# Decoder layer on one core: the causal mask of the maxima moves from a matmul into VectorE's reduction, and the heads' own blocks are masked on VectorE

## The chip, the cores and the metric

The kernel runs on one core of a Trainium2 chip. The metric is the device time of one execution in microseconds (us), the median of several runs. A core has five engines, each with a queue of its own that is worked off in order: TensorE (PE in the profile; PEld is its loading of weights), VectorE (DVE), ScalarE (ACT), GpSimd (POOL) and SyncE (SP), which here only starts transfers (DMAs). They wait for each other by semaphores. SBUF is the working memory, PSUM the one that matmuls write, in eight banks of 512 float32 columns.

## The reference

One decoder layer over x [8, 512, 256]: attention over tokens, attention over heads within each token, and a linear layer, each behind a layer norm and added to x. The weights' quantisation and the low-rank part belong to the linear layer and are not touched here.

```python
# 1. causal attention over tokens, 16 heads; real and imaginary halves together make 32 dimensions
scores = (q_r @ k_r^T + q_i @ k_i^T) / sqrt(16)
scores = where(tril(ones(N, N)), scores, -inf)
probs  = softmax(scores);  out = probs @ v;  x = x + out @ Wo
# 2. attention over the heads of one token, with q = layernorm(x), k = v = ctx
scores = einsum('bsqd,bskd->bsqk', qh, kh) / sqrt(16)          # 16 x 16 for each token
scores = where(tril(ones(16, 16)), scores, -1e18)
x = x + softmax(scores) @ vh
# 3. x = x + layernorm(x) @ w + bias + low rank part
```

## The kernel before

Eight batches (N_BATCH) of 512 tokens go through a software pipeline. The body is written out for the first turns and the last, and is a loop for those between; each turn has four passes `g`, one for each group of G = 4 heads, and each pass has ten units `n`. All engines run the same `body(i, g, n)` order, each with its own part. In one pass TensorE works on several groups at once: it projects q and k of group A (three ahead), takes the maxima of group B (two ahead, shifted by SHIFT = 1 unit, so that the last unit of a group falls to n = 0 of the next pass), turns the maxima of group M, and computes the exponentials' scores and the weighted values of group C. Batch-wide work (output projection, transposes, layer norms, the linear layer) is hung on single passes, so that one pass in four is longer.

The softmax needs the largest score of each query before the exponentials. So scores are computed twice. For the maxima, queries lie on the partitions: a unit of `QUERY_UNITS` fills one bank of 512 columns with one block of 512 (four units), two blocks of 384 and 128 (four units) or two of 256 (two units). At the end of each unit one more matmul adds the mask: `mask_q` (through the unit matrix `ident_b`, bf16) is added to the one or two diagonal blocks of 128 columns. The function is `scores`, L589 to L604, used for both sides. VectorE then takes the maxima, `take_max`, L1190 to L1201: one TENSOR_REDUCE for each bank. Since a bank with blocks of 384 and 128 columns is reduced in four segments of 128, the three parts of block 2 go to `seg_max`, and after the last unit VectorE waits for itself, joins them by a small reduction (L1259) and a copy (L1260), and tells TensorE by `max_ready`. TensorE turns the 16 maxima of each query into rows (`turn_maxima`, L626), ACT copies them to `max_row` (L943), and a DMA puts them as an extra row into `stack_q`. There are two banks for the maxima (`max_bank0`, `max_bank1`), and TensorE waits with unit n until VectorE has taken unit n - 2.

The operands of both score matmuls lie in `stack_q` and `stack_k`. They are filled by six DMAs of 256 KB for each group from SyncE's queue (L443 to L461): q_hi twice, q_lo, k_hi twice, k_lo, where ACT copies the high part from PSUM and VectorE makes the low part (`low_part`, L1203 to L1208). TensorE waits for all six before unit 0.

The attention over heads is spread over GpSimd and VectorE, a tile of 128 tokens a pass (26 tiles in this way, the others in the end part). GpSimd multiplies (L311), VectorE sums into `head_scores` (L1213, at n = 5 and n = 8), GpSimd adds `head_mask` over 256 columns into `head_probs` (L1580), VectorE takes `head_max` (L1330, n = 9), GpSimd subtracts it (L1583), ACT exponentiates (L931), VectorE sums and inverts, GpSimd normalises (L1565) and multiplies with the values (L1570), VectorE sums and adds to x2 (L1296).

## Time and profile before

| | |
|---|---|
| median of 3 runs | 827.26 us (824.56 to 828.38) |
| profiled execution, its own time | 829.26 us |
| its span, first to last instruction | 827.4 us |
| granted TensorE clock, mean | 0.971 of full speed |
| PE busy | 759.1 us (92%) |
| DVE busy | 628.8 us (76%) |
| POOL busy | 489.6 us (59%) |
| ACT busy | 402.8 us (49%) |

The profile shows one execution. Busy time is the union of an engine's instructions. Matmuls are pipelined and their ends are modelled, so a busy TensorE isn't TensorE at its peak; the distance from the start of one matmul to the start of the next says more. The first 44 us are start-up, the maxima of groups are taken from 34 to 697 us, and the last 100 us are the end part of the last batches.

### The profile page before, as it was taken

Reading aid. Unit: us, or ns where it says so; the run is one execution under the profiler, and the core shown is the slowest. Engines: PE = TensorE matmul, PEld = TensorE weight load, DVE = VectorE, ACT = ScalarE, POOL = GpSimd, SP = SyncE. Lnnn points to the kernel's source line nnn. Section 1 sums busy time; section 2 is a strip of 40 time slices with the busy share of each in tenths; the row PEclk is TensorE's granted clock in tenths of the full one; section 3 lists DMA queues with packets and bytes.
Section 4 is the critical chain, followed back from the end, with each engine's and each line's share of the span. In section 5 each row is a group of like instructions: output and inputs, shape, how many; then the busy total and the mean of one; then the engine's idle time right before and its main releaser. Section 6 shows DMA issues by size and latency. Waiting matters only on the chain.

```text
span 827.4 us, 15883 instructions
## 1 busy us (share of the span) xinstructions
PE 759.1 (92%) x5563; PEld 520.8 (63%) x5563; DVE 628.8 (76%) x1225; ACT 402.8 (49%) x760; POOL 489.6 (59%) x452
## 2 busy tenths in 40 slices
PE   3688999999999999999999999999999998998997
PEld 2565655765566556666666666665766564587995
DVE  2544555457768998899879987999798879789873
ACT  5114555555555566545646573647464546541111
POOL 5000000031966799678958786878787888976541
PEclk9658999999999999999999999999999999999997
DMA  5886656866686668566646675667566760100001
GB/s 180 111 105 82 98 78 84 135 84 84 84 135 78 90 84 134 70 91 107 90 94 90 103 93 100 90 104 95 76 87 107 100 93 8 58 14 8 32 14 38
DMA packets 47980, 70.54 MB, mean 85 GB/s; under 512 B 4897, under 2 KB 22578, under 8 KB 47922
## 3 DMA queue, kind: packets, MB, share of 16 engines
q1 hardware_dynamic: 46898, 69.52, 56.1%
q8 instruction: 34, 0.56, 0.4%
q10 hardware_dynamic: 1024, 0.26, 0.1%
q14 instruction: 24, 0.20, 0.1%
HBM read 14.98 MB, written 4.19 MB: 23 GB/s over the span
## 4 chain that ended last, share of the span: by engine, by line
PE 58%; DMA 15%; DVE 13%; POOL 5%; issue 4%; ACT 2%; SPq 1%; DVEq 0%; ACTq 0%; POOLq 0%
PE misc L518 21%; DMA stack_k<-k_lo 14%; PE exp_bank L518 14%; PE acc_bank L518 9%; PE max_bank L518 9%; PE sum_bank L518 3%; POOL prod L1570 3%; DVE neg_max L1201 2%; DVE seg_max L1201 2%; DVE x L1296 2%; SPq L449 1%; POOL prod L311 1%; DVE head_scores L1213 1%; DVE head_out L1213 1%; DVE ln_raw L1179 1%
## 5 line engine op out<-in xcount | busy, mean ns | idle before, releaser
L927 ACT ACTIVATE probs<-exp_bank 128x512 f32<-128x512 f32 x320 | 188.4, 592 | 204.0 <-PE exp_bank L518 201.1
L1201 DVE TENSOR_REDUCE neg_max<-max_bank 128x1 f32<-128x512 f32 (+1 forms) x192 | 130.6, 683 | 93.0 <-PE max_bank L518 92.4
L1570 POOL TENSOR_TENSOR prod<-head_probs,ctx_sb 128x256 f32<-128x256 f32 (+1 forms) x100 | 185.1, 1882 | 2.2 <-POOL head_probs L1565 0.5
L518 PE MATMUL max_bank<-stack_k,stack_q 96*128 96x384 f32 (+3 forms) x512 | 158.2, 372 | 17.2 <-DMA stack_k<-k_lo 9.1
L518 PE MATMUL acc_bank<-probs,values 128*32 128x512 f32 (+3 forms) x1024 | 157.6, 445 | 4.6 <-ACT log_sum L938 2.6
L311 POOL TENSOR_TENSOR prod<-x1n,ctx_sb 128x256 f32<-128x256 f32 (+1 forms) x104 | 158.4, 1554 | 4.3 <-ACT x1n L887 4.3
L518 PE MATMUL sum_bank<-probs,ones 128*32 128x512 f32 (+3 forms) x1024 | 156.9, 442 | 0.0
L518 PE MATMUL exp_bank<-stack_q,stack_k 97*128 97x384 f32 (+3 forms) x512 | 150.0, 355 | 2.1 <-DVE wf_lo L1171 1.3
L1512 POOL TENSOR_TENSOR ln_var<-ln_mv,eps 128x4 f32<-128x4 f32 x21 | 4.5, 213 | 198.3 <-DVE ln_mv L1187 198.3
L518 PEld LDWEIGHTS exp_bank<-stack_q,stack_k 97*128 97x128 f32 x512 | 84.1, 194 | 56.2 <-issue 28.2
L1201 DVE TENSOR_REDUCE seg_max<-max_bank 128x4 f32<-128x512 f32 x128 | 86.7, 682 | 28.2 <-PE max_bank L518 27.0
L518 PEld LDWEIGHTS max_bank<-stack_k,stack_q 96*128 96x128 f32 x512 | 88.8, 204 | 23.4 <-DMA stack_k<-k_lo 8.6
L518 PE MATMUL max_bank<-mask_q,ident_b 128*128 128x256 bf16 (+1 forms) x320 | 86.7, 271 | 0.0
L518 PE MATMUL exp_bank<-mask_k,ident_b 128*128 128x256 bf16 (+1 forms) x320 | 84.8, 265 | 0.0
L1213 DVE TENSOR_REDUCE head_scores<-prod 128x64 f32<-128x1024 f32 (+1 forms) x104 | 79.6, 805 | 4.0 <-POOL prod L311 4.0
L1213 DVE TENSOR_REDUCE head_out<-prod 128x64 f32<-128x256 f32 (+2 forms) x100 | 74.7, 804 | 0.0
L518 PE MATMUL misc<-xt_hi,w_hi 128*128 128x512 f32 x128 | 57.8, 451 | 14.8 <-ACT max_row L880 12.5
L518 PEld LDWEIGHTS acc_bank<-probs,values 128*32 128x32 f32 x1024 | 39.0, 108 | 45.3 <-issue 27.0
L518 PE MATMUL exp_bank<-prod,ident 128*128 128x160 f32 (+4 forms) x416 | 61.0, 307 | 2.4 <-POOL prod L356 2.4
L518 PEld LDWEIGHTS exp_bank<-prod,ident 128*128 128x128 f32 x416 | 58.9, 190 | 4.0 <-POOL prod L356 2.5
L518 PEld LDWEIGHTS exp_bank<-mask_k,ident_b 128*128 128x128 bf16 x320 | 31.3, 98 | 36.6 <-issue 26.2
L518 PE MATMUL misc<-wo_sb,attn_t 128*128 128x256 f32 x224 | 51.3, 382 | 1.4 <-DVE xt_lo L1312 1.3
(181 smaller groups left out, 1360.2 us busy)
## 6 DMA issues: line engine op xcount, KB each, us to landing
stack_q<-q_hi SPq DMA_DIRECT2D x64, 256.0 KB, 5.6
stack_k<-k_hi SPq DMA_DIRECT2D x64, 256.0 KB, 9.6
stack_q<-q_lo SPq DMA_DIRECT2D x32, 256.0 KB, 7.0
stack_k<-k_lo SPq DMA_DIRECT2D x32, 256.0 KB, 10.7
x_in<-in_x SPq DMA_DIRECT2D x9, 512.0 KB, 4.7
ctx_sb<-in_ctx SPq DMA_DIRECT2D x32, 128.0 KB, 3.3
x<-in_x SPq DMA_DIRECT2D x7, 512.0 KB, 10.1
out<-y_sb SPq DMA_DIRECT2D x5, 512.0 KB, 3.3
```

Of the source, the lines that this page charges most:

```text
L311: last = engine.tensor_tensor(qk_prod[:, COFF[j]:COFF[j + 1]].rearrange("p (q k d) -> p q k d", q=4, d=HD), x1n[:, t, 4 * j * HD:4 * (j + ...
L449: sp.dma_start(to[n * D:(n + 1) * D, s, :, :].bitcast(F32), part[:, :].bitcast(F32)).then_inc(stacked, 16)
L518: return nc.tensor.matmul(*args, **kw)
L927: nc.scalar.activation(probs[:, (UNITS * g + n) % PTR, :], exp_bank[n % 2][:, :], ACT.Exp, scale=SCALE).then_inc(exp_done, 1)
L1179: last = vec.bn_stats(ln_raw[:, which, t, :], src[:, t, :])
L1201: vec.tensor_reduce(o, v, axis=AX_X, op=ALU.max, negate=True).then_inc(max_taken, 1)
L1213: last = vec.tensor_reduce(out(j), products(j), axis=AX_X, op=ALU.add)
L1296: vec.tensor_tensor(x2[:, t, :], x2[:, t, :], head_out[:, :], ALU.add).then_inc(x2_ready, 1)
L1512: own(gp.tensor_tensor(ln_var[:, which, :], ln_mv[:, which, :, 1], eps[:, :], ALU.add))
L1570: last = gp.tensor_tensor(pv_prod[:, COFF[j]:COFF[j + 1]].rearrange("p (q d k) -> p q d k", q=4, k=keys), head_probs[:, 4 * j:4 * j + 4, N ...
```

## The change

The mask matmul of the query side goes. `take_max` now has one instruction for each block: it adds `causal` (zeros, with the triangle in the last 128 columns) to the block, writes the sum back to the bank and keeps the maximum, straight into `query_max`. `seg_max`, the small reduction, the copy and `max_ready` go; the maxima are no longer negated, and ACT's copy to `max_row` gets scale -1. In the attention over heads the entries of later chunks of keys hold the mask's value from the start, and VectorE adds the mask to the heads' own 4 x 4 blocks (`own_heads`, 64 columns) where GpSimd added it over all 256.

```diff
-            def scores(bank, unit, lhs, rhs, slot, rows, key_side, done):
+            def query_scores(bank, unit, slot):
+                for h, blk, at, width in unit[0]:
+                    last = mm(bank[:, at:at + width], stack_q[0:STACK, slot, h, blk * P:(blk + 1) * P],
+                              stack_k[0:STACK, slot, h, 0:width], start=True, stop=True, skip_group_check=True)
+                last.then_inc(max_scored, 1)
+            def key_scores(bank, unit, slot):
                 parts, (col, count, step) = unit
                 for n, (h, blk, at, width) in enumerate(parts):
-                    first = blk * P if key_side else 0
-                    mm(bank[:, at:at + width], lhs[0:rows, slot, h, blk * P:(blk + 1) * P],
-                       rhs[0:rows, slot, h, first:first + width], start=(n == 0), stop=False,
+                    mm(bank[:, at:at + width], stack_k[0:STACK + 1, slot, h, blk * P:(blk + 1) * P],
+                       stack_q[0:STACK + 1, slot, h, blk * P:blk * P + width], start=(n == 0), stop=False,
                        skip_group_check=True)
...
             def turn_maxima(slot):
-                pe.wait_ge(max_ready, n_max_ready.up())
+                pe.wait_ge(max_taken, n_max_ready.up(UNITS))
...
-                            copy(max_row[:, m_slot % 2, :], misc[0][0:G * NT, 0:P]).then_inc(max_row_ready, 1)
+                            nc.scalar.activation(max_row[:, m_slot % 2, :], misc[0][0:G * NT, 0:P], ACT.Identity,
+                                                 scale=-1.0).then_inc(max_row_ready, 1)
...
             def take_max(n, ring):
-                dve.wait_ge(max_scored, n_scored.up())
+                wait_apart(dve, const_ready, (max_scored, n_scored.up()))
                 bank = max_bank[n % 2]
-                if n < G:
-                    o, v = neg_max[:, ring, n:n + 1, 3], bank[:, :]
-                elif n < 2 * G:
-                    o, v = seg_max[:, n - G, :], bank[:, :].rearrange("p (s k) -> p s k", k=P)
-                else:
-                    h = 2 * (n - 2 * G)
-                    o, v = neg_max[:, ring, h:h + 2, 1], bank[:, :].rearrange("p (s k) -> p s k", k=2 * P)
-                vec.tensor_reduce(o, v, axis=AX_X, op=ALU.max, negate=True).then_inc(max_taken, 1)
+                for h, blk, at, width in QUERY_UNITS[n][0]:
+                    v = bank[:, at:at + width]
+                    last = vec.tensor_tensor_reduce(v, v, causal[:, T - width:T], 1.0, -3.0e38, ALU.add, ALU.max,
+                                                    query_max[:, ring, h, blk:blk + 1])
+                last.then_inc(max_taken, 1)
...
-                            if unit == UNITS - 1:
-                                dve.wait_ge(max_taken, n_scored.now())
-                                vec.tensor_reduce(neg_max[:, ring, :, 2], seg_max[:, :, 0:3], axis=AX_X, op=ALU.min)
-                                vec.tensor_copy(neg_max[:, ring, :, 0], seg_max[:, :, 3]).then_inc(max_ready, 1)
...
                             dve.wait_ge(hqk_prod, n_prod.up())
-                            wait(dve, h_masked, n_masked.up() - 1)
+                            wait(dve, h_shifted, n_shifted.up() - 1)
                             score_sums((3,))
...
+                        if scored and n == 9:
+                            dve.wait_ge(hqk_sum, n_masked.up())
+                            vec.tensor_tensor(own_heads, own_heads, head_mask[:, None, 0:4, 0:4]
+                                              .to_broadcast([P, CHUNKS, 4, 4]), ALU.add).then_inc(h_masked, 1)
...
-                            vec.tensor_reduce(head_max[:, :], head_probs[:, :, :], axis=AX_X,
+                            vec.tensor_reduce(head_max[:, :], head_scores[:, :, :], axis=AX_X,
...
-            own(gp.memset(head_scores[:, :, :], 0.0))
+            for j in range(CHUNKS - 1):
+                last = gp.memset(head_scores[:, 4 * j:4 * j + 4, 4 * (j + 1):], MASKED)
+            own(last)
...
-                        pool.wait_ge(hqk_sum, n_sum.up())
                         wait(pool, hpv_prod, n_attended.up() - 1)
-                        gp.tensor_tensor(head_probs[:, :, :], head_scores[:, :, :], head_mask[:, :, :],
-                                         ALU.add).then_inc(h_masked, 1)
                         pool.wait_ge(h_max, n_max.up())
-                        gp.tensor_tensor(head_probs[:, :, :], head_probs[:, :, :],
+                        gp.tensor_tensor(head_probs[:, :, :], head_scores[:, :, :],
                                          head_max[:, :, None].to_broadcast([P, NH, NH]),
                                          ALU.subtract).then_inc(h_shifted, 1)
```

## Rows read from the trace of the kernel before

**Rows 1.** Windows of one pass each: from:to length, busy us (instructions) by engine, clock, DMA.

```profile
171.65:190.43 18.78, 17.82 (x142) 11.18 (x141) 11.53 (x22) 11.63 (x23) 7.63 (x8) 1.00 0.72 92
...
339.70:359.20 19.50, 18.66 (x151) 11.97 (x151) 18.20 (x36) 12.87 (x25) 15.43 (x15) 1.00 0.67 89
359.20:380.70 21.50, 20.77 (x168) 14.08 (x167) 19.90 (x38) 10.08 (x20) 14.48 (x12) 1.00 0.68 106
380.70:399.90 19.20, 18.06 (x144) 11.25 (x143) 17.95 (x37) 12.02 (x24) 16.98 (x18) 1.00 0.66 90
399.90:427.00 27.10, 25.63 (x184) 17.95 (x183) 21.26 (x34) 13.69 (x27) 21.52 (x16) 1.00 0.62 102
```

**Rows 2.** Timeline of TensorE: start us, us, engine, line, what.

```profile
401.46 0.39 PE L518 MATMUL misc<-xt_hi,w_lo 128*128 128x512 f32 x1
401.69 0.40 PE L518 MATMUL exp_bank<-stack_q,stack_k 97*128 97x512 f32 x1
...
403.83 0.48 PE L518 MATMUL max_bank<-stack_k,stack_q 96*128 96x512 f32 x1
404.16 0.23 PE L518 MATMUL max_bank<-mask_q,ident_b 128*128 128x128 bf16 x1
404.20 0.48 PE L518 MATMUL exp_bank<-stack_q,stack_k 97*128 97x384 f32 x2
...
404.56 0.48 PE L518 MATMUL max_bank<-stack_k,stack_q 96*128 96x384 f32 x2
404.88 0.28 PE L518 MATMUL max_bank<-mask_q,ident_b 128*128 128x256 bf16 x1
405.10 0.62 PE L518 MATMUL acc_bank<-probs,values 128*32 128x512 f32 x2
```

**Rows 3.** The chain that ended last, and the longest waits (us in total, times, longest).

```profile
385.62 10.13 DMA stack_k<-k_lo
...
395.87 0.56 PE max_bank L518 x2
...
PE max_bank L518 <- DMA stack_k<-k_lo: 9.1, 11, 2.3
```

**Rows 4.** DMA issues of the page: count, KB each, median us to landing.

```profile
stack_k<-k_lo SPq DMA_DIRECT2D x32, 256.0 KB, 10.7
```

**Rows 5.** Timelines of SyncE's queue and of TensorE: the last issue, its first reader.

```profile
363.58 0.55 SPq L449 DMA_DIRECT2D stack_k<-k_lo  x1
...
376.70 0.47 PE L518 MATMUL max_bank<-stack_k,stack_q 96*128 96x512 f32 x1
...
403.93 0.55 SPq L449 DMA_DIRECT2D stack_k<-k_lo  x1
...
422.94 0.48 PE L518 MATMUL max_bank<-stack_k,stack_q 96*128 96x512 f32 x1
```

**Rows 6.** Groups by form, VectorE: count | busy us, mean ns | idle before.

```profile
L1201 DVE TENSOR_REDUCE neg_max<-max_bank 128x1 f32<-128x512 f32 x128 | 86.8, 681 | 62.0 <-PE max_bank L518 61.7
L1207 DVE TENSOR_TENSOR k_lo<-misc,k_hi 128x512 fp32r<-128x512 f32 x32 | 21.8, 680 | 4.4 <-ACT k_hi L880 4.4
L1296 DVE TENSOR_TENSOR x<-x,head_out 128x256 f32<-128x256 f32 x24 | 28.6, 1190 | 0.0
L1260 DVE COPY neg_max<-seg_max 128x4 f32<-128x4 f32 x32 | 15.0, 470 | 0.0
L1259 DVE TENSOR_REDUCE neg_max<-seg_max 128x4 f32<-128x12 f32 x32 | 5.4, 168 | 1.1
L1415 DVE TENSOR_TENSOR x_in<-x_in,exp_bank 128x256 f32<-128x256 f32 x4 | 1.7, 418 | 5.8 <-PE exp_bank L518 5.8
```

**Rows 7.** Timelines of VectorE and GpSimd around one addition to x2.

```profile
365.54 2.33 DVE L1296 TENSOR_TENSOR x<-x,head_out 128x256 f32<-128x256 f32 x1
367.79 0.68 DVE L1201 TENSOR_REDUCE seg_max<-max_bank 128x4 f32<-128x512 f32 x1
...
363.14 7.47 POOL L1570 TENSOR_TENSOR prod<-head_probs,ctx_sb 128x256 f32<-128x256 f32 x4
```

More of the change, by code:

```diff
@@ L151, in decoder_layer @@
         wo_sb = sb("wo_sb", [P, NG, C])
-        seg_max = sb("seg_max", [P, G, NT])
-        neg_max = sb("neg_max", [P, 2, G, NT])
+        query_max = sb("query_max", [P, 2, G, NT])
         max_row = sb("max_row", [G * NT, 2, P], F32R)
@@ L171, in decoder_layer @@
         qk_prod, pv_prod = prod[:, 0, :], prod[:, 1, :]
-        head_scores = sb("head_scores", [P, NH, NH])
+        score_rows = sb("score_rows", [P, (NH + 1) * NH])
+        head_scores = score_rows[:, 0:NH * NH].rearrange("p (q k) -> p q k", k=NH)
+        own_heads = score_rows.rearrange("p (j s) -> p j s", j=CHUNKS)[:, :, 0:4 * NH] \
+            .rearrange("p j (q k) -> p j q k", k=NH)[:, :, :, 0:4]
         head_probs = sb("head_probs", [P, NH, NH])
@@ L188, in decoder_layer @@
         ident_b = sb("ident_b", [P, P], BF16)
-        mask_q = sb("mask_q", [P, P], BF16)
+        causal = sb("causal", [P, T], BF16)
         mask_k = sb("mask_k", [P, P], BF16)
@@ L499, in _ @@
             n_stack, n_row = turn.count(16 * STACK_DMAS * NG), turn.count(16 * NG)
-            n_max_bank, n_max_ready = turn.count(UNITS * NG), turn.count(NG)
+            n_max_bank, n_max_ready = turn.count(UNITS * NG), turn.count(UNITS * NG)
             n_exp_bank, n_probs, n_v = turn.count(UNITS * NG), turn.count(UNITS * NG), turn.count(NG)
@@ L587, in project_v @@
                 last.then_inc(v_psum, 1)
[L589 removed]
+            def query_scores(bank, unit, slot):
[4 more added lines that the diff above has]
+            def key_scores(bank, unit, slot):
                 parts, (col, count, step) = unit
                 for n, (h, blk, at, width) in enumerate(parts):
[L593 to L595 removed]
+                    mm(bank[:, at:at + width], stack_k[0:STACK + 1, slot, h, blk * P:(blk + 1) * P],
+                       stack_q[0:STACK + 1, slot, h, blk * P:blk * P + width], start=(n == 0), stop=False,
                        skip_group_check=True)
[L597 removed]
                 if count == 1:
[L599 removed]
+                    o, m = bank[:, col:col + P], mask_k[:, :]
                 else:
                     o = bank[:, :].rearrange("p (a n) -> p a n", n=P)[:, col // P:col // P + step // P + 1:step // P, :]
[L603 to L604 removed]
+                    m = mask_k[:, None, :].to_broadcast([P, 2, P])
+                mm(o, ident_b[:, :], m, start=False, stop=True, skip_group_check=True).then_inc(exp_scored, 1)
             def attend(units, slot, first_tile):
@@ L682, in body @@
                             wait(pe, exp_done, n_exp_bank.up() - 2)
-                            scores(exp_bank[n % 2], KEY_UNITS[n], stack_k, stack_q, st["C"][1], STACK + 1,
-                                   True, exp_scored)
+                            key_scores(exp_bank[n % 2], KEY_UNITS[n], st["C"][1])
                         if stack_early(i, g) and n == 1 and (i, g) != FIRST_PASS:
@@ L696, in body @@
                             wait(pe, max_taken, n_max_bank.up() - 2)
-                            scores(max_bank[unit % 2], QUERY_UNITS[unit], stack_q, stack_k, slot, STACK,
-                                   False, max_scored)
+                            query_scores(max_bank[unit % 2], QUERY_UNITS[unit], slot)
                         if st["N"] and n == 1:
@@ L1113, in _ @@
             n_wo, n_y, n_yb = turn.count(CC), turn.count(CC), turn.count(1)
-            n_prod, n_masked, n_exp = turn.count(NT), turn.count(NT), turn.count(NT)
+            n_prod, n_shifted, n_masked, n_exp = (turn.count(NT), turn.count(NT), turn.count(NT),
+                                                  turn.count(NT))
             n_pv, n_kept, n_norm = turn.count(NT), turn.count(1), turn.count(NT)
@@ L1496, in _ @@
             n_ctx = [turn.count(16) for _ in range(NT)]
-            n_qk, n_sum, n_max = turn.count(NT), turn.count(NT), turn.count(NT)
+            n_qk, n_max = turn.count(NT), turn.count(NT)
             n_inv, n_pv, n_attended = turn.count(NT), turn.count(NT), turn.count(NT)
@@ L1520, in _ @@
             gp.memset(ident[:, :], 0.0)
-            gp.memset(mask_q[:, :], 0.0)
+            gp.memset(causal[:, :], 0.0)
             gp.memset(mask_k[:, :], 0.0)
@@ L1530, in _ @@
                                  pattern=[[-1, P]], channel_multiplier=1))
-            gp.affine_select(out=mask_q[:, :], in_=mask_q[:, :], compare_op=ALU.is_ge, fill=MASKED, base=0,
+            gp.affine_select(out=causal[:, T - P:T], in_=causal[:, T - P:T], compare_op=ALU.is_ge, fill=MASKED, base=0,
                              pattern=[[-1, P]], channel_multiplier=1)
@@ L1633, in _ @@
             gp.memset(end_shift, MASKED).then_inc(end_preset, 1)
-            pool.wait_ge(hqk_sum, n_sum.now())
+            pool.wait_ge(hqk_sum, n_qk.now())
             end_pool_scores(2)
```

8 lines of the change are left out of this document (2 added, 6 removed).

## The prediction

> **What bounds the kernel now.** I read the page's busy times first, which put TensorE far ahead of VectorE. They are averages, so I cut the loop into passes (one pass is one turn of the g loop over ten units) and asked for the busy time of each [rows 1]. A pass lasts 18.8 to 21.5 us, and every fourth one 27 us. TensorE has work for 94 to 97% of each. VectorE starts at 11.5 of 18.8 us in an early pass, but in the second half of the loop it has 18.0 of 19.2 us: nearly full in the short passes, with room only in the long one (21.3 of 27.1).
>
> Matmuls are pipelined, so I read the price of a mask matmul from starts, not from durations [rows 2]. Then I read the chain of waits and the waits for DMAs, which show something that the busy shares hide [rows 3]. The first unit of maxima of a pass needs the six copies into stack_q and stack_k, and the last of them lands late. In one short pass k_lo is issued at 385.62 us, needs 10.13 us, and the matmul starts at 395.87, which was the landing. TensorE waited for this transfer 11 times. Its median time is 10.7 us [rows 4]. In other passes it lands early: issued at 363.58 it has landed by about 374.3, and its first reader starts at 376.70; issued at 403.93 it has landed by about 414.6, and the reader starts at 422.94 [rows 5]. Reading all 32 passes this way (the 32 issues are the one row of [rows 4]) I find 15 of 31 intervals with 1.6 to 8 us of margin, and 16 with 0 to 0.8 us, on average 0.25 us. So TensorE's work sets about half of the passes, and the loop projection, copies, six DMAs, first unit sets the others at about 19 us: from 376.70 to 395.87 is 19.2 us.
>
> **Mask matmuls on the query side (removed).** Ten a pass, 320 in all. A whole unit of one 512-wide block: matmul at 403.83, mask at 404.16, next matmul at 404.20, so 0.37 us. A 512-wide matmul with no mask behind it passes TensorE on in 0.23 us (401.46 to 401.69). The mask thus costs about 0.13 us, more than its own 128 columns, because it also leaves too little time to load the next weights. A unit of two blocks: 404.56, mask at 404.88, next at 405.10, where the next one waits for the array to drain. Of these 0.22 us about half is the mask's 256 columns and half is the draining, which stays; I take 0.10 us. Per pass 4 x 0.13 + 6 x 0.10 = 1.1 us. The bounds: 0.04 us each (the shortest start to start in these rows), 0.4 us a pass; and the full durations, 4 x 0.23 + 6 x 0.28 = 2.6 us a pass, which double-counts what overlaps.
>
> **What of it arrives.** In the 15 loose passes all of it: 15 x 1.1 = 16.5 us. In the 16 tight ones TensorE would arrive early at a transfer that doesn't land earlier. Only the mask of the first unit lies inside the loop between first unit and next projection, about 0.15 us, and to it comes the margin that the pass had, 0.25 us: 16 x 0.4 = 6.4 us. Together 23 us. The stall that TensorE is then late for is again the landing of k_lo.
>
> **VectorE's maxima (changed).** Before: 10 reductions of 512 columns, 0.68 to 0.69 us each [rows 6]. After: 16 instructions for the same 5120 columns, four of 512, four pairs of 384 and 128, four of 256. The new instruction reads a bank and causal, writes the bank back and keeps a maximum; the trace has none. Its nearest row is a TENSOR_TENSOR of PSUM and SBUF: 680 ns for 512 columns, 418 ns for 256 [rows 6], so 1.02 ns a column on 0.157 us fixed. Durations: 4 x 0.68 + 4 x (0.55 + 0.29) + 4 x 0.42 = 7.76 us against 6.8 us. Back to back, two instructions overlap by 0.08 us (one of 2.33 us starts at 365.54, the next at 367.79 [rows 7]), which takes 6 x 0.08 off: +0.45 us a pass. Unknown is a surcharge a for the custom program with its kept maximum and for writing the bank that is being read. Lower end 0. Upper end a whole extra short instruction, 168 ns (L1259) [rows 6]. I take 0.03 us, near the low end, as the instruction streams each column once like its nearest row; 16 x 0.03 = 0.5 us.
>
> The Trainium skill bears on this price. Its page "Vector Engine (DVE) Microarchitecture Reference", section "Measured stream behaviour on trn2", says that programs of several micro-operations paid the same fixed time per instruction as built-in ones, about 75 ns after overlap. By that rule a is 0 and the forecast would be about 3 us lower; no row here shows a custom instruction.
>
> **The hand-over (removed).** The small reduction (168 ns) and the copy of four columns (470 ns on average) go once a pass, and with them a wait of VectorE for itself: about -0.5 us of VectorE a pass. The copy is that slow for so little because it can be held up by GpSimd, which the next part explains.
>
> **The heads' own blocks (moved from GpSimd to VectorE).** 26 tiles. VectorE gets an addition of 64 columns, both inputs in SBUF: 0.157 + 64 x 1.02 = 0.22 us, back to back 0.14. But such an addition can stand still while GpSimd works. The row for x2 plus head_out (256 columns, two SBUF inputs) has a mean of 1190 ns, against 418 ns for the same width from PSUM [rows 6], and one of 2.33 us starts at 365.54 in the middle of GpSimd's products, which run from 363.14 for 7.47 us [rows 7]. The extra is 0.77 us on average. I charge 0.4 us, as the new addition comes at n = 9, where GpSimd has often finished its products and waits for head_max. Bounds 0 and about 2 us. GpSimd's addition over 256 columns goes, and head_max no longer waits for it. GpSimd is nowhere near full in these passes except the long one (21.5 of 27.1 us [rows 1]), so I cost its gain at nothing.
>
> The Trainium skill speaks against this part: "SBUF — State Buffer", section "Who interferes with whom", says that a VectorE instruction with two SBUF inputs and a GpSimd instruction that reads SBUF exclude each other for their whole length. By it every overlap costs up to the rest of one GpSimd instruction. The trace agrees (2.33 us against 0.42).
>
> **VectorE's sum.** Per pass +0.45 + 0.5 - 0.5 + 0.14 + 0.4 = +1.0 us. The short passes leave 19.2 - 18.0 = 1.2 us and the long ones 5.8 us [rows 1]. So it fits, but with no air: now and then a maximum will be taken late and, with two max banks, TensorE waits for it. I charge 0.16 us for each of 31 passes, 5 us. Queued behind such a late maximum on VectorE are q_lo and k_lo; their DMAs are issued 6 to 10 us before they are served, so a lag of a microsecond there costs nothing.
>
> **At nothing:** the sign of the maxima moves into ACT's copy (same instruction with a scale); the longer memset of causal and the three strided ones run while GpSimd waits for the first statistics; one more wait on a long-past semaphore per unit. After the last unit of maxima (about 697 us) nothing changes.
>
> **Sum.** 829.3 us (the profiled execution's own time, span 827.4) - 23 + 5 = 811. The median of the runs is 2.0 us under the profiled execution, so 809 us is forecast.
>
> **Rivals.** (1) VectorE becomes the bound, and the kernel slower. With a at 168 ns a pass needs 0.5 + 16 x 0.168 = 3.2 us more of VectorE: 21.2 and 21.4 us in passes of 19.2 and 19.5, 23.1 in 21.5, while the long pass still shortens by 1.1. That is +4.4 us in four passes, over the some 20 full ones +22 us at most; the early passes and the long ones' reserves give back 10 to 14. About 838 us. It decides from about a = 0.12 us. For it: no row shows the instruction. Against: its nearest relatives cost 680 ns like the reduction. (2) All of TensorE's gain arrives and VectorE costs nothing: 31 x 1.1 = 34 us, 793 us. Against it are the 11 waits for k_lo. (3) The gain is eaten between the tight transfer and small waits of both engines on each other, 823 to 831 us: this is what it would be if the masks cost their lower bound, 31 x 0.4 = 12 us, less 5 and a bit more for VectorE.
>
> **Chances.** Forecast (798 to 819 us) 0.60; rival 1 0.15; rival 2 0.10; rival 3 0.15. By 0.5% (4 us, about what a measurement of this kernel can tell from no change): rival 3 gives 0.12 of its 0.15 to no change. Faster 0.73, same 0.12, slower 0.15. The range 790 to 834 us takes in rival 2, rival 3 and the beginning of rival 1.
>
> **What would show it.** Right: no mask_q matmul; a 512-wide unit passed on in about 0.23 us; pass lengths of about 19 us unchanged where the k_lo wait was, with that wait longer and more often; the long passes near 26 us; TENSOR_TENSOR_REDUCE rows of about 0.71, 0.58, 0.32 and 0.45 us. Wrong: those rows above 0.8 us for 512 columns; VectorE busy at 98% in short passes with TensorE waiting for it; or additions of own_heads of 1 us and more.

## The result, and the profile after

The changed kernel takes 830.68 us (median of 22 runs, 826.20 to 837.27), the kernel before 828.03 us (22 runs on the same chip, 824.56 to 838.33). The ratio is 1.0038, with a 95% interval of 1.0022 to 1.0054: no gain, and if anything a loss of 3 us. The forecast was 809 us.

The first lines are the page of the changed kernel: busy times, and the queue that brings instructions.

```profile
PE 738.0 (89%) x5243; PEld 505.2 (61%) x5243; DVE 638.3 (77%) x1891; ACT 398.7 (48%) x760; POOL 471.7 (57%) x428
...
q14 instruction: 39, 0.32, 0.2%
```

TensorE lost 21 us of its 759.1 busy us and the kernel is not shorter. VectorE grew from 628.8 to 638.3 us. Its groups by form answer to [rows 6]:

```profile
L1203 DVE CUSTOM_DVE_ANT_0 max_bank<-max_bank,causal 128x512 f32<-128x512 f32 x128 | 88.7, 697 | 69.1 <-PE max_bank L520 68.2 <-DVE prod L1166 0.2
L1203 DVE CUSTOM_DVE_ANT_0 max_bank<-max_bank,causal 128x384 f32<-128x384 f32 x128 | 72.3, 565 | 17.4 <-PE max_bank L520 17.3
L1203 DVE DVE_READ_ACCUMULATOR2_ANT query_max<- 128x1 f32 x512 | 71.8, 140 | 0.0
L1203 DVE CUSTOM_DVE_ANT_0 max_bank<-max_bank,causal 128x256 f32<-128x256 f32 x128 | 51.6, 444 | 29.3 <-PE max_bank L520 23.7 <-issue 5.4
L1203 DVE CUSTOM_DVE_ANT_0 max_bank<-max_bank,causal 128x128 f32<-128x128 f32 x128 | 42.1, 329 | 0.0
...
L1295 DVE TENSOR_TENSOR x<-x,head_out 128x256 f32<-128x256 f32 x24 | 18.7, 781 | 0.0
...
L1311 DVE TENSOR_TENSOR score_rows<-score_rows,head_mask 128x64 f32<-128x64 f32 x26 | 11.8, 452 | 0.0
```

The new maxima last 697, 565, 329 and 444 ns, near the forecast's 710, 580, 320 and 450. Each of the 512 is followed by a second instruction, a read of the accumulator. And one form has an idle time put down to "issue", 5.4 us: VectorE waited for no semaphore there. The waits say how often (us in total, times, longest):

```profile
PEld max_bank L520 <- DVE query_max L1203: 24.5, 35, 2.4
PE max_bank L520 <- DVE query_max L1203: 14.8, 27, 2.0
PE max_bank L520 <- DMA stack_k<-k_lo: 10.5, 12, 1.9
...
DVE max_bank L1203 <- issue: 5.4, 2, 2.7
```

The wait for k_lo is about as it was (12 times, 10.5 us; before 11 times, 9.1 us [rows 3]). TensorE now waits 27 times for VectorE's maxima, 14.8 us in all (before 12 times, 7.8 us). Three passes in a row (columns as in [rows 1]) show a gain in one, none in the next, and a loss in the long one:

```profile
351.63:371.43 19.80, 19.37 (x158) 13.29 (x157) 17.26 (x55) 10.33 (x20) 13.34 (x8) 1.00 0.64 82
371.43:390.53 19.10, 17.29 (x134) 10.67 (x133) 18.36 (x58) 11.98 (x24) 16.11 (x15) 1.00 0.78 125
390.53:421.06 30.53, 26.18 (x172) 18.13 (x172) 23.15 (x58) 13.77 (x27) 24.46 (x20) 0.94 0.55 92
```

The same passes of the kernel before take 21.4, 19.2 and 27.1 us. Only two passes are of the 30 us kind. Their beginning, on VectorE's timeline:

```profile
390.01 0.42 DVE L1333 TENSOR_REDUCE head_max<-score_rows 128x16 f32<-128x256 f32 x1
393.16 0.43 DVE L1203 CUSTOM_DVE_ANT_0 max_bank<-max_bank,causal 128x256 f32<-128x256 f32 x1 [2.73 <-issue]
...
479.65 0.42 DVE L1333 TENSOR_REDUCE head_max<-score_rows 128x16 f32<-128x256 f32 x1
482.75 0.43 DVE L1203 CUSTOM_DVE_ANT_0 max_bank<-max_bank,causal 128x256 f32<-128x256 f32 x1 [2.69 <-issue]
```

Between the two instructions of each pair lies the jump back of the software pipeline's loop. The loop runs three times and jumps back twice; in the trace VectorE's compare-and-branch starts at 390.09 and 479.74 us, and its next instruction follows 2.8 us later. In the kernel before that takes 0.3 us (394.99 to 395.33).

The queue that brings instructions points to a fetch. From 390 to 397 us, which begins with the first jump, the changed kernel's view of the DMA queues has three packets of it (packets, MB, share of the 16 DMA engines), and one of the three falls into the 2.8 us:

```profile
q14 instruction: 3, 0.02, 1.2%
```

In the kernel before, from 394 to 402 us, around its first jump, only two other queues move anything:

```profile
q1 hardware_dynamic: 188, 0.22, 10.0%
q10 hardware_dynamic: 32, 0.01, 0.4%
```

The same holds over a whole turn, from 388 to 480 us: five packets on queue 14 in the changed kernel, none in the kernel before. The view does not name the engine that a packet is for, so that VectorE stood waiting for one of them is argued from the times.

On TensorE the same moment reads:

```profile
391.37 0.63 PE L520 MATMUL sum_bank<-probs,ones 128*32 128x256 f32 x8
394.16 0.27 PE L636 MATMUL misc<-ident,query_max 128*16 128x128 f32 x1 [2.17 <-DVE query_max L1203]
394.87 0.80 PE L520 MATMUL misc<-xt_hi,w_hi 128*128 128x512 f32 x1 [0.44 <-ACT max_row L948]
395.46 0.63 PE L520 MATMUL misc<-xt_lo,w_hi 128*128 128x512 f32 x1
...
397.17 0.63 PE L520 MATMUL misc<-xt_hi,w_lo 128*128 128x512 f32 x1
```

TensorE has nothing to do for 2.17 us, and after that its matmuls of 512 columns last 0.63 us and start 0.43 us apart, where they otherwise last 0.39 and start 0.23 apart. The clock confirms it (windows; the last three columns are the granted clock, the DMA share and GB/s):

```profile
390.53:394.10 3.57, 1.47 (x17) 0.59 (x17) 0.94 (x5) 0.45 (x2) 3.41 (x6) 1.00 0.03 7
394.10:397.60 3.50, 3.00 (x8) 2.24 (x8) 3.45 (x6) 0.86 (x2) 3.50 (x4) 0.54 0.02 5
397.60:400.00 2.40, 2.40 (x13) 1.55 (x11) 1.39 (x4) 2.08 (x5) 2.40 (x2) 0.95 0.06 23
```

After the idle stretch the grant is 0.54 for 3.5 us, almost the lower of the two levels (1.2 instead of 2.4 GHz). 3.5 us at 0.54 are worth 1.6 us, so a start that is 2.7 us late on VectorE becomes some 4.3 us in the pass; the version written out, below, puts it at 4.5 and 4.7 us.

### The profile page after: what moved, and what is told of

It is laid out like the page before. It is cut to its first block, busy times and chain, and to the rows that moved or that the text cites. A ratio compares the mean times of both kernels' runs of the same rounds, so it can differ in the third digit from the quotient of the medians.

```text
span 828.7 us, 16167 instructions
## 1 busy us (share of the span) xinstructions
PE 738.0 (89%) x5243; PEld 505.2 (61%) x5243; DVE 638.3 (77%) x1891; ACT 398.7 (48%) x760; POOL 471.7 (57%) x428
## 4 chain that ended last, share of the span: by engine, by line
PE 49%; DVE 18%; DMA 12%; issue 9%; POOL 8%; ACT 2%; SPq 1%; DVEq 0%; POOLq 0%; ACTq 0%
PE misc L520 19%; PE exp_bank L520 12%; DMA stack_k<-k_lo 12%; PE acc_bank L520 7%; DVE max_bank L1203 6%; PE max_bank L520 5%; POOL prod L313 3%; PE sum_bank L520 3%; POOL prod L1575 3%; DVE score_rows L1217 2%; DVE ln_raw L1186 2%; DVE query_max L1203 1%; ACT max_row L948 1%; DVE attn_t L1298 1%; PE misc L636 1%
## 5 line engine op out<-in xcount | busy, mean ns | idle before, releaser
L1203 DVE CUSTOM_DVE_ANT_0 max_bank<-max_bank,causal 128x384 f32<-128x384 f32 (+3 forms) x512 | 242.1, 509 | 115.7 <-PE max_bank L520 109.2
L520 PE MATMUL max_bank<-stack_k,stack_q 96*128 96x384 f32 (+3 forms) x512 | 158.9, 374 | 25.5 <-DVE query_max L1203 14.8
L520 PE MATMUL exp_bank<-stack_q,stack_k 97*128 97x384 f32 (+3 forms) x512 | 146.8, 349 | 4.7 <-ACT probs L932 2.6
L1217 DVE TENSOR_REDUCE score_rows<-prod 128x64 f32<-128x1024 f32 (+1 forms) x104 | 79.9, 808 | 8.7 <-POOL prod L313 8.7
L1203 DVE DVE_READ_ACCUMULATOR2_ANT query_max<- 128x1 f32 x512 | 71.8, 140 | 0.0
L1584 POOL TENSOR_TENSOR head_probs<-score_rows,head_max 128x256 f32<-128x256 f32 x26 | 16.3, 626 | 91.6 <-DVE head_max L1333 91.6
L520 PEld LDWEIGHTS exp_bank<-mask_k,ident_b 128*128 128x128 bf16 x320 | 31.4, 98 | 37.3 <-issue 27.5
```

The lines of the kernel that those rows point to most:

```text
L520: return nc.tensor.matmul(*args, **kw)
L1203: last = vec.tensor_tensor_reduce(v, v, causal[:, T - width:T], 1.0, -3.0e38, ALU.add, ALU.max, query_max[:, ring, h, blk:blk + 1])
L1217: last = vec.tensor_reduce(out(j), products(j), axis=AX_X, op=ALU.add)
L1584: gp.tensor_tensor(head_probs[:, :, :], head_scores[:, :, :], head_max[:, :, None].to_broadcast([P, NH, NH]), ALU.subtract).then_inc(h_shi ...
```

## The experiments

My theory after this reading (A): VectorE's loop body became too long to jump back cheaply, and that eats some 9 us. Rivals: (B) the new instructions cost the gain by themselves, spread over all passes; later (C): not the length but the place of the loop in the instruction stream matters.

**The changed kernel, written out.** All turns of the pipeline are written out instead of looped, on all engines.

```diff
         def batches(self, eng, body, n_batch):
-            first, after = 3, n_batch - 2
-            for i in range(-1, first):
-                body(i, i)
...
-            with eng.Fori(first, after) as reg:
...
+            for i in range(-1, n_batch):
+                body(i, i)
```

> The changed kernel with its batches written out instead of the loop over batches 3 to 5, on all engines. Theory A: the changed kernel loses 8 to 10 us at the loop's two jumps back, where VectorE starts 2.7 us late and TensorE then idles and runs slow; so this takes about 820 us and has no gap of more than 0.5 us on VectorE for which nothing in the profile is to blame. Theory B: the accumulator reads (512 times some 60 ns of VectorE) hold TensorE up all along and the jumps are hidden; then it stays at 829 to 831 us.

Measured 821.21 us, ratio 0.9897 (0.9869 to 0.9926). The same three passes as above:

```profile
351.60:371.40 19.80, 19.45 (x158) 13.34 (x157) 17.35 (x55) 10.34 (x20) 13.48 (x8) 1.00 0.62 82
371.40:390.20 18.80, 17.24 (x134) 10.63 (x133) 18.18 (x58) 11.67 (x24) 16.12 (x14) 1.00 0.79 127
390.20:416.20 26.00, 24.53 (x172) 17.18 (x172) 21.70 (x59) 14.05 (x27) 24.17 (x20) 1.00 0.64 107
```

The two 30 us passes last 26.0 us each at full clock, and the others are as in the changed kernel. The two jumps cost 4.5 and 4.7 us in the passes: 9.3 us together, 9.5 us by the medians of the two kernels, 11.7 us by their ratios. Rival B alone is out: all new instructions are still there, and a gain of 1.0% is back. What they do cost, about 8 us, is measured further down.

**The kernel before, written out**, by the same edit.

> The kernel before with its batches written out. Its jumps cost 0.3 us each in its trace, so both theories expect 826 to 828 us, no difference from the kernel before. If instead writing out costs or gives something by itself, the gain of the changed kernel written out must be read against this one.

829.07 us, ratio 0.9998 (0.9982 to 1.0015). Writing out is worth nothing to a kernel whose jumps are cheap.

**The kernel before with one more wait for each maximum** (the wait that the change added, without its new instruction).

```diff
             def take_max(n, ring):
-                dve.wait_ge(max_scored, n_scored.up())
+                wait_apart(dve, const_ready, (max_scored, n_scored.up()))
```

> The kernel before, with one more wait on a long-past semaphore ahead of each maximum (wait_apart in take_max), as the changed kernel has it: VectorE's loop body grows from 238 recorded instructions to about 278, the changed kernel's has 362. If the late start after a jump comes from the length of the body, and the limit lies below 278, the two jumps now take 2.7 us each and the kernel takes 833 to 837 us. If the limit lies above 278, or the waits themselves cost nothing and length is not the cause, it stays at 828 us.

829.67 us, ratio 1.0009 (0.9985 to 1.0033). The body has 278 instructions instead of 238 (counted between two branches in the trace), and the jump still takes 0.3 us. The waits themselves cost nothing that these runs can tell (less than 0.4%).

**The kernel before without the query side's masks.** The mask matmuls are left out and nothing replaces them, so the maxima are taken over masked scores too. It bounds what the change could bring to TensorE.

```diff
             def scores(bank, unit, lhs, rhs, slot, rows, key_side, done):
                 parts, (col, count, step) = unit
+                if not key_side:
+                    for h, blk, at, width in parts:
+                        last = mm(bank[:, at:at + width], lhs[0:rows, slot, h, blk * P:(blk + 1) * P],
+                                  rhs[0:rows, slot, h, 0:width], start=True, stop=True, skip_group_check=True)
+                    last.then_inc(done, 1)
+                    return
```

> The kernel before with the mask matmul of the query side left out and VectorE untouched; the maxima are then taken over masked scores too, that is the part left out. It measures what TensorE's part alone is worth. The prediction's sum says -23 us: 804 to 806 us. A rival, that the six transfers bind more passes than it counted, says -10 us: 818 us.

813.24 us, ratio 0.9797 (0.9769 to 0.9824). By the ratio that is -16.8 us (-15.5 by the medians of this series), and not the 23 forecast. Its windows:

```profile
348.40:368.20 19.80, 19.37 (x156) 13.28 (x155) 17.71 (x37) 10.24 (x20) 14.57 (x11) 1.00 0.63 82
368.20:387.20 19.00, 17.06 (x133) 10.56 (x132) 18.06 (x37) 12.11 (x25) 17.63 (x17) 1.00 0.80 125
```

The pass that has no wait for a transfer falls from 21.4 to 19.8 us, the tight one stays at 19.0. In this profile one accident has the size of a jump: pass 22 took 30.5 us. The timelines of VectorE and of GpSimd show the main part of it.

```profile
484.96 3.99 DVE L1302 TENSOR_TENSOR x<-x,head_out 128x256 f32<-128x256 f32 x1
488.88 0.67 DVE L1305 TENSOR_TENSOR attn_t<-acc_sb,misc 128x512 f32<-128x512 f32 x1
...
483.63 5.04 POOL L1576 TENSOR_TENSOR prod<-head_probs,ctx_sb 128x768 f32<-128x768 f32 x2
```

An addition of 256 columns stood for 3.99 us beside GpSimd's products, attn_t came late, and TensorE waited 2.01 us for it. The granted clock over this pass was 0.89, and two stretches make that up (windows, the grant is the third number from the end):

```profile
473.00:476.50 3.50, 3.50 (x9) 2.52 (x10) 1.54 (x4) 1.25 (x3) 3.50 (x4) 0.51 0.01 2
490.10:493.50 3.40, 3.40 (x24) 1.81 (x23) 3.40 (x8) 1.19 (x2) 0.67 (x1) 0.50 0.94 272
```

Only the second follows the blocked addition. The first lies before it, behind a wait of 1.21 us for a maximum at the start of the pass. So this pass shows the same chain by another cause (a late VectorE, an idle TensorE, a lower grant) for a part of its 5 us.

**The strips alone, written out** (the new maxima, the heads' part as before), and **the same with the mask matmuls kept too**, so that the two differ only in TensorE's work. The cut shows the second against the first.

```diff
             def query_scores(bank, unit, slot):
-                for h, blk, at, width in unit[0]:
...
-                              stack_k[0:STACK, slot, h, 0:width], start=True, stop=True, skip_group_check=True)
-                last.then_inc(max_scored, 1)
+                for n, (h, blk, at, width) in enumerate(unit[0]):
...
+                       stack_k[0:STACK, slot, h, 0:width], start=(n == 0), stop=False, skip_group_check=True)
+                col, count, step = unit[1]
...
```

> The changed kernel written out, with the attention over heads as in the kernel before (GpSimd adds the mask over 256 columns): only the maxima are changed. If the moved addition of the heads' own blocks costs VectorE what its rows say (26 times 0.45 us) and it is on the path, this is 3 to 6 us faster than the changed kernel written out, 815 to 818 us. If GpSimd's shorter chain gives as much back, it is the same, 820 to 822 us.

> As the one before it, but TensorE keeps its mask matmul (the mask is then added twice, which changes nothing in the maxima): VectorE's dearer maxima alone, with no gain of TensorE. If their 3 us a pass of VectorE are mostly taken from its idle time, 829 to 833 us; if VectorE is full in three passes of four, 838 to 845 us.

819.47 us (ratio 0.9879, 0.9831 to 0.9926) and 836.82 us (1.0068, 1.0035 to 1.0100); both lie between the two values that were set against each other, so neither of those questions is answered by them. The difference, 17.4 us (15.6 by the ratios), is the masks' worth a second time, though less cleanly: in the profile of the slower one pass 24 took 27.0 us instead of 21.4, an accident that may not be in every run. The strips written out against the run with no mask at all: 819.47 - 813.24 = 6.2 us (6.8 by the ratios, with a margin of about 4.6 us from the two intervals) is what VectorE's dearer maxima cost.

**The heads' part alone**, in the kernel before.

```diff
+                        if scored and n == 9:
+                            vec.tensor_tensor(own_heads, own_heads, head_mask[:, None, 0:4, 0:4]
+                                              .to_broadcast([P, CHUNKS, 4, 4]), ALU.add).then_inc(h_masked, 1)
...
-                        gp.tensor_tensor(head_probs[:, :, :], head_scores[:, :, :], head_mask[:, :, :], ALU.add)
```

> The kernel before with only the second part of the change: VectorE masks the heads' own blocks, GpSimd no longer adds the mask. GpSimd is freed of 0.67 us a tile, VectorE has 0.45 us more, and its wait for GpSimd goes. The sum of the prediction (+0.5 us a pass for VectorE, hidden in its idle time) says no change, 826 to 830 us; if the tiles' chain over GpSimd sets passes, 822 to 825 us.

826.40 us, ratio 0.9960 (0.9929 to 0.9992): a gain of 3 us by itself. But the full change written out is 1.7 us slower than the strips written out. Those two intervals overlap widely, so its sign inside the full change is not settled; it is small either way.

**The kernel before with a long body.** Four long-past waits ahead of each maximum; nothing else of the change.

```diff
             def take_max(n, ring):
-                dve.wait_ge(max_scored, n_scored.up())
+                for _ in range(3):
+                    dve.wait_ge(const_ready, 1)
+                wait_apart(dve, const_ready, (max_scored, n_scored.up()))
```

> The kernel before with four more waits on a long-past semaphore ahead of each maximum: VectorE's loop body has about 398 recorded instructions, where one wait gave 278 and no late start. If the length of the body is what makes VectorE start 2.7 us late after a jump back, both jumps show it and the kernel takes 834 to 840 us. If the custom instruction or its tables are the cause, the jumps stay at 0.3 us and the kernel takes 828 to 832 us.

838.40 us, ratio 1.0109 (1.0046 to 1.0171). Two waits each went into one instruction, so the body has 323 instructions, not the 398 expected. It is enough:

```profile
393.59 0.42 DVE L1332 TENSOR_REDUCE head_max<-head_probs 128x16 f32<-128x256 f32 x1 [0.19 <-POOL head_probs L1582]
396.88 0.69 DVE L1203 TENSOR_REDUCE neg_max<-max_bank 128x2 f32<-128x512 f32 x1 [2.87 <-issue]
```

Passes 18 and 22 last 31.2 and 31.4 us, against 27.1 and 26.1. The kernel before, with none of the new instructions, gets the changed kernel's fault.

**Strips only where they are cheap.** One block of 512 needs one new instruction for one old; two blocks need two for one. So the four single units get the new maxima, the six others keep mask matmul and reduction.

```diff
             def take_max(n, ring):
+                if n < G:
+                    wait_apart(dve, const_ready, (max_scored, n_scored.up()))
+                    vec.tensor_tensor_reduce(bank[:, :], bank[:, :], causal[:, :], 1.0, -3.0e38, ALU.add, ALU.max,
+                                             neg_max[:, ring, n, 3:4]).then_inc(max_taken, 1)
+                    return
                 dve.wait_ge(max_scored, n_scored.up())
```

> The kernel before with the new maxima only for the four units that hold one block of 512 columns: there the mask matmul goes and VectorE's instruction adds causal; the six units of two blocks keep the mask matmul and one reduction. The heads' part, the small reduction with its copy and the loop are as before. Sum by rows: TensorE saves 4 x 0.13 = 0.5 us in each loose pass; VectorE pays 4 x 0.02 us for the longer main instruction and up to 4 x 0.14 us for the accumulator reads, 0.1 to 0.6 us a pass. Theory A (what costs is the length of VectorE's loop body): the body grows from 238 recorded instructions to about 254 and stays under the limit between 278 and 323, so no 2.8 us at the jumps, and the ratio is 0.990 to 0.998 (820 to 826 us). Rival B (the new instruction itself costs more than its row shows, through the bank it writes or through the clock): half of what the full change costs over its gain, ratio 1.000 or above.

820.57 us, ratio 0.9855 (0.9809 to 0.9901), better than theory A said (0.990 to 0.998). The body has 270 instructions. Its passes:

```profile
351.80:372.30 20.50, 20.07 (x164) 13.77 (x163) 17.98 (x41) 10.53 (x20) 14.79 (x11) 1.00 0.60 80
372.30:391.40 19.10, 17.84 (x140) 11.08 (x139) 18.17 (x41) 11.73 (x24) 16.93 (x16) 1.00 0.81 125
391.40:417.30 25.90, 25.33 (x178) 17.69 (x178) 20.52 (x39) 13.78 (x27) 24.90 (x21) 1.00 0.65 107
```

The first of them shortened by 1.0 us, though only four masks went, worth 0.5 by my price. Unit by unit, the single units gave 0.08, 0.14, 0.08 and 0.14 us, 0.44 together, and unit 5, whose masks stayed, 0.54 us. There the kernel before has a small wait, and the mixed one has none. First the kernel before, TensorE's timeline in the stretch of [rows 7]; then the mixed kernel, VectorE's timeline at the same unit:

```profile
368.52 0.50 PE L518 MATMUL max_bank<-stack_k,stack_q 96*128 96x384 f32 x2 [0.29 <-DVE seg_max L1201]
```

```profile
361.83 0.39 DVE L1309 TENSOR_TENSOR x<-x,head_out 128x256 f32<-128x256 f32 x1
362.14 0.68 DVE L1214 TENSOR_REDUCE seg_max<-max_bank 128x4 f32<-128x512 f32 x1
```

Before, the addition to x2 meets GpSimd's products and takes 2.33 us [rows 7]; the maximum behind it comes late, and TensorE waits. In the mixed kernel the same addition takes 0.39 us. A small shift of phase took away a wait that has nothing to do with masks.

**The same with the heads' part**, looped and written out.

> As the mixed kernel, with the heads' part of the change too; the loop is kept. Theory A: if the recorded body stays under about 278 instructions the heads' part adds what it gave alone (ratio 0.996), so 0.986 to 0.995 (816 to 824 us). If the body passes the limit, both jumps cost 2.8 us of VectorE and passes 18 and 22 last 30.5 us and more, and the ratio is 0.998 to 1.006. Rival B (no limit, only a sum of small costs): ratio about 1.000 with no late start of VectorE at the jumps.

> The same kernel with the turns of the pipeline written out instead of a loop, so that no length of a body can matter. Theory A: no late start of VectorE anywhere, and the ratio is that of the looped one if its body stayed under the limit (0.986 to 0.995), 0.009 to 0.012 lower if it did not. Against the full change written out (0.990): equal within 0.005, as half of TensorE's saving goes with most of VectorE's extra work.

820.70 us (0.9864, 0.9811 to 0.9916) and 820.83 us (0.9855, 0.9806 to 0.9905). The body has 274 instructions, the jumps take 0.3 us, and so writing out gives nothing that shows; the heads' part gives nothing here either.

**No mask, and five transfers instead of six.** k_lo is not stacked (its rows of stack_k are zero); so this leaves out the mask of the maxima and the k_lo term of the scores.

```diff
-                        stack(stack_k, 2, k_lo)
...
+            vec.memset(stack_k[2 * D:3 * D, :, :, :].bitcast(F32), 0.0)
```

> The kernel before with no mask on the query side (maxima over masked scores too, VectorE's reductions as before) and with the sixth transfer of each group left out: k_lo is not stacked, its rows of stack_k are zero. The loop is kept. What it leaves out: the mask of the maxima, and the k_lo term of the scores. It tells what holds the tight passes. If it is the landing of the last of six transfers (my reading of the waits in the kernel before), the passes that stay at 19.0 us with no mask matmul now shorten to what TensorE or VectorE needs, 17.5 to 18.5 us, and the ratio falls from 0.980 to 0.955 to 0.970. If something else holds them (VectorE's 18 us, or ACT's copies ahead of the transfers), they stay within 0.3 us of 19.0 and the ratio stays within 0.977 to 0.983.

798.37 us, ratio 0.9595 (0.9537 to 0.9653).

```profile
337.10:356.90 19.80, 19.37 (x157) 13.27 (x157) 17.72 (x37) 10.25 (x20) 14.57 (x11) 1.00 0.52 68
356.90:374.40 17.50, 16.79 (x133) 10.48 (x132) 16.88 (x35) 11.39 (x23) 16.68 (x15) 1.00 0.70 114
```

The pass bound by TensorE stays at 19.8 us; the tight one, which no saving on TensorE had moved below 18.8, falls to 17.5. The transfers hold it.

**Length or place?** The cheap jumps so far ended at places 649, 778, 788 and 811 of VectorE's stream, the dear ones at 1012 and 1180 (counted in the program). The place could have been the reason, so three runs move the loop and keep its body. (The cut shows the first of them.)

```diff
+            ahead = [90]        # 440 in the changed kernel, 240 in the one with the long body
             def take_max(n, ring):
+                for _ in range(1):      # 4 and 2
+                    if ahead[0] > 0:
+                        ahead[0] -= 1
+                        dve.wait_ge(const_ready, 1)
```

> The kernel before with 90 waits on a long-past semaphore ahead of maxima in the turns before the loop (78 more instructions ahead of it); the body keeps its 238 instructions. The loop stands at places 489 to 727 of VectorE's stream, 727 being 215 modulo 256. Theory A (length of the body decides): both jumps take 0.3 us, passes 18 and 22 last 26 to 27 us. Rival C (place decides): VectorE starts 2.7 us late at both jumps and passes 18 and 22 last 30.5 us or more.

> The changed kernel with 440 such waits ahead of the loop (220 more instructions); the body keeps its 362. The loop stands at 1038 to 1400, 1400 being 120 modulo 256. Theory A: as the changed kernel, VectorE 2.7 us late at both jumps, passes 18 and 22 at 30.5 us, ratio 1.003 to 1.008. Rival C: no late start, passes 18 and 22 at 26 us, ratio 0.988 to 0.994 like the version written out, at the loop's size.

> The kernel before with the four long-past waits ahead of each maximum (body of 323 instructions), and 240 further waits ahead of the loop (120 more instructions). The loop stands at 809 to 1132, 1132 being 108 modulo 256. Theory A: late by 2.8 us at both jumps, passes 18 and 22 at 31 us. Rival C: no late start, passes 18 and 22 at 26 to 27 us.

The short body, moved: 827.42 us in its one run, the jumps take 0.3 us, passes 18 and 22 last 27.1 and 26.1 us. The changed kernel, moved: 829.88 us, ratio 1.0031 (1.0009 to 1.0053), passes 18 and 22 last 30.8 us each:

```profile
392.17 0.42 DVE L1338 TENSOR_REDUCE head_max<-score_rows 128x16 f32<-128x256 f32 x1
395.32 0.43 DVE L1208 CUSTOM_DVE_ANT_0 max_bank<-max_bank,causal 128x256 f32<-128x256 f32 x1 [2.73 <-issue]
```

The other long body, moved: 842.14 us in its one run, passes 18 and 22 last 31.3 us each. The short body stayed cheap and both long ones stayed dear, so a shift by itself changes nothing at these three places, and theory A forecast all three.

Rival C is not wholly out. The short body was moved only to 727, and no cheap jump ends beyond 811 while no dear one ends before 1012. A short body at the long ones' places was not run, and neither was a version in which length and place could act together.

## Why the prediction was wrong

**The step that failed** stands under "at nothing": "one more wait on a long-past semaphore per unit". I priced each added instruction by its own time, which for the waits is indeed nothing that shows (the kernel before with more waits: 1.0009). I did not count the loop's body, neither there nor for the 16 maxima a pass. The waits brought 40 instructions and the accumulator reads that go with the 64 new maxima 64 more; with the changes around them the body went from 238 to 362. The waits alone do not make the difference: without them it would still be 322, one less than a body that was dear. Between 278 and 323 instructions the jump back of this loop goes from 0.3 to 2.8 us. The queue that starts late was the very one on which TensorE's next work hangs (turn_maxima waits for the last unit), and the idle stretch was followed by half the clock. That is 9.3 us in two passes; in the sum it had no term, and no rival named it.

The jumps are about half of the miss. The forecast was -23 + 5 = -18 us, the kernel moved by +3.1 us by the ratio. Of these 21 us, 11.7 are the jumps by the ratios, 6.2 are masks that did not pay, and 3.3 are VectorE's work above its charge. These shares carry the margins given with the sum below. Without the jumps the kernel takes 821.21 us, which is still above the forecast's 798 to 819 us.

The Trainium skill, page "Runtime: NRT & Kernel Launch", section "Instruction fetch mechanics", says that an engine holds two blocks of 16 KiB, 256 instructions each, and that a jump to a target outside them waits for a fetch. The trace agrees that such a wait exists, and the instruction packets point to a fetch (23 to 26 on queue 14 with the short bodies, 38 to 40 with the long ones). It does not agree with the size: with two blocks of 256 in line, no offset of the stream puts all the short bodies inside and all the long ones outside, and 323 is far below 512. The packets on queue 14 are smaller, about 8 KB (39 packets, 0.32 MB). An estimate from this and from that page's 256 instructions to 16 KiB is 128 instructions a packet. With three blocks of 128 in reach, 58 of the 128 possible offsets sort all the looped versions rightly. By that reading the place would matter together with the length: 323 instructions would be cheap at some places and 278 dear at others. No run tests it, so the bound from 278 to 323 holds for the places that were run.

**Mask matmuls, 1.1 us a pass: right.** In the pass of 21.4 us the single units gave 0.44 us and the pairs 0.64, 1.08 us together (forecast 0.5 and 0.6). The pass shortened by 1.65 us, since the wait behind the x2 addition went as well.

**What of it arrives, 23 us: 16.8 measured.** The tight passes were to give 0.4 us each. Over passes 3, 4, 7 to 9, 11 to 13, 17, 21, 25 and 29 the run without masks gave 0.3 us in all: ten of them 0.24 us each on average, while passes 9 and 13 grew by 1.0 and 1.2 us. The trace shows what happened there. With less work TensorE came to the late transfer earlier and stood idle for 1.66 and 1.58 us before the passes began; within both a stretch at half the clock followed, which no pass of the kernel before shows while it takes maxima, from 73 us on (windows):

```profile
200.00:203.40 3.40, 3.04 (x8) 2.15 (x7) 0.00 (x0) 0.30 (x2) 3.40 (x2) 0.50 0.01 2
285.30:288.70 3.40, 3.04 (x8) 2.15 (x7) 1.80 (x4) 0.27 (x1) 3.40 (x2) 0.50 0.01 2
```

Such a stretch is worth 1.7 us; pass 10, a loose one, has one too (from 220.5 us) and grew by 1.3 us. The sum had no term for the clock. That the transfers hold these passes was right, and is now shown by the run with five of them (19.0 to 17.5 us).

**VectorE's extra work, charged 5 us for maxima, hand-over and heads' part together: about 8 measured.** The maxima with the hand-over cost 6.2 to 6.8 us, and with the heads' part it is 821.21 - 813.24 = 8.0 us (8.3 by the ratios). The main instruction costs 16 ns more than the reduction of 512 columns (697 against 681), inside the 30 ns of a. The accumulator's read is a second instruction of 140 ns; its start is recorded together with that of the next instruction, so most of it lies beside that. The Trainium skill has this rule, which I did not use: "VectorE: DVE Perf Modes", section "Two Vector instructions with no wait between them", says that an operation that also writes out its accumulator is two instructions. The trace agrees (512 of 512), and it matters twice, since it is also two places of a loop's body. By the page named in the forecast a was 0; that is near for the main instruction and leaves out the read.

**Rival 1, VectorE becomes the bound:** not by its instructions. TensorE waits for its maxima 27 times, but in the version without jumps it waits 25 times and the gain is there. **Rival 3, the gain is eaten,** gave the right number (823 to 831) by luck: it needed masks worth 0.4 us a pass, they were worth 1.1, and two jumps ate the rest.

**The heads' blocks:** the addition of 64 columns lasts 452 ns on average (0.22 where nothing meets it), and the addition to x2 fell from 1190 to 781 ns. That is phase rather than this part: in the mixed kernel, where GpSimd keeps its additions, it is 765. Alone this part is worth 3 us; I had charged it 0.4 us a pass.

The sum in place of mine, in ratios to the kernel before: masks -2.0%, maxima +0.8%, heads' part +0.2%, jumps +1.4%, together +0.4%. The four terms are differences between neighbouring kernels and the sum closes by their construction; each is uncertain by about 0.3% (masks, jumps) to 0.6% (maxima, heads' part).

## What to carry to other kernels

Count the instructions that a change puts into an engine's loop, waits and accumulator reads too, before pricing them; an edit that is free by duration can bring a loop to where each jump back costs microseconds. An idle time that ends on "issue" right where a loop closes is the sign, and writing the loop out is the test. And try a new instruction first only where it replaces one for one: the mixed version, with four of ten units changed, keeps the loop and beats both kernels (0.9855). Against the full change written out (0.9897) the intervals overlap, and half of what the mixed one gained in the pass shown came from a shift of phase.

## What the runs showed of the hardware

The jump back of a loop on VectorE took 0.3 us with 238, 242, 270, 274 and 278 instructions in the body and 2.8 us (once 3.0) with 323 and 362. The first ended at places 649 to 811 of its stream, the others at 1012 to 1400; a version between 278 and 323, and a short body at the later places, were not run. From 405 to 478 us, inside one turn of the loop, each of the four versions with a long body has instruction packets in its trace, and none of the eight with a short body has any.

Idle stretches of 1.6 to 2.2 us on TensorE were followed by a lower granted clock: 0.54 over the 3.5 us after a jump, 0.50 over the 3.4 us behind the blocked addition, and 0.50 over 3.4 us in passes 9 and 13 without masks. Behind the jump and the blocked addition a pass of about 26 us became one of 30.5. It is not so behind every one: in the kernel before TensorE stood idle for 2.43 us from 744.8 us on, and the grant stayed at 1.00 (windows):

```profile
744.80:747.30 2.50, 0.07 (x3) 0.03 (x1) 2.50 (x6) 2.37 (x5) 2.42 (x5) 1.00 0.00 0
747.30:750.80 3.50, 3.50 (x26) 3.50 (x27) 3.40 (x8) 0.69 (x2) 1.31 (x1) 1.00 0.02 5
```
